# Graph attention on one core: order of the residual chain and of the finished rows in the last turns

## The reference

```python
x = _layernorm(x + L0(x))     # two GraphSAGE steps with mean over neighbours
# L1: attention over the edges, four heads of 128
alpha = einsum('ehd,ehd->eh', q[dst], k[src] + e) / sqrt(D)
attn = softmax of alpha over the edges of one destination
out = segment_sum((v[src] + e) * attn) + (x @ Wskip + bskip)
normed = (out - mu) * rsqrt(var + LN_EPS) * ln_g + ln_b
x = _layernorm(x + elu(normed @ Wlin + blin + x))
```

## Time and profile before

| what | value |
|---|---|
| median of 3 runs | 1611.04 us |
| lowest and highest run | 1610.73 and 1617.06 us |
| the profiled execution's own time | 1612.87 us |
| its span | 1610.7 us |
| mean granted clock of TensorE | 0.977 of full speed |

### The profile page before, as it was taken

One profiled execution on the slowest core, in us unless ns is written; L12 is line 12 of the kernel. 1 busy time (PEld: TensorE's weight loads), 2 busy tenths in 40 slices (PEclk: granted clock), 3 DMA queues, 4 the chain that ended last, 5 costly groups with the idle time before them and its releaser, 6 DMA issues. The chain is left out here.

```text
span 1610.7 us, 35668 instructions
## 1 busy us (share of the span) xinstructions
PE 1483.8 (92%) x8869; PEld 1135.5 (70%) x8869; DVE 1326.6 (82%) x6248; ACT 1169.2 (73%) x3273; POOL 1036.0 (64%) x1038
## 2 busy tenths in 40 slices
PE   4999999999999998999699977999999999999973
PEld 3777777777777776788566643777777777777763
DVE  5999999999999998566468865788888888888873
ACT  2999999999999998344257751677777777777763
POOL 3788888878888885677367727466566556655421
PEclk9999999999999999999989998999999999999997
DMA  2566666554444443233269963233333333333210
GB/s 80 147 161 159 159 162 162 155 159 150 150 150 150 152 150 119 73 92 92 58 197 288 291 214 97 81 91 91 90 89 87 88 91 90 90 90 88 67 41 6
DMA packets 148429, 199.22 MB, mean 124 GB/s; under 512 B 28399, under 2 KB 71582, under 8 KB 148310
## 3 DMA queue, kind: packets, MB, share of 16 engines
q1 hardware_dynamic: 119690, 160.01, 32.5%
q0 software_dynamic: 27200, 36.26, 10.0%
q10 hardware_dynamic: 1420, 1.60, 0.3%
HBM read 106.66 MB, written 100.07 MB: 128 GB/s over the span
## 5 line engine op out<-in xcount | busy, mean ns | idle before, releaser
L1371 POOL DMA_INDIRECT big<-x_tab,look x196 | 199.8, 1019 | 92.3 <-issue 58.6
L739 PEld LDWEIGHTS pb<-MG_s,big 128*128 128x128 f32 x832 | 149.5, 189 | 126.7 <-ACT big L772 110.5
L1388 POOL DMA_INDIRECT out_dram<-big,idx x98 | 100.5, 1026 | 210.6 <-PE pb L1466 73.4
L739 PE MATMUL pb<-MG_s,big 128*128 128x256 f32 x832 | 207.3, 392 | 24.7 <-ACT big L772 24.6
L748 ACT ACTIVATE big<-big 128x128 f32<-128x128 f32 x416 | 180.2, 482 | 0.0
L721 PE MATMUL pb<-C_s,big 128*128 128x128 f32 x832 | 161.8, 276 | 0.0
L722 PE MATMUL pb<-Ws1c_s,big 128*128 128x128 f32 x832 | 161.8, 276 | 0.0
L880 POOL TENSOR_TENSOR big<-big,cl 128x512 f32<-128x512 f32 x104 | 133.3, 1282 | 36.1 <-DVE big L844 34.0
L1689 DVE CUSTOM_DVE_ANT_0 big<-pb,big,zero 128x128 f32<-128x128 f32 x392 | 119.6, 345 | 38.7 <-PE pb L1511 38.3
L1442 PEld LDWEIGHTS pb<-big 128*128 128x128 f32 x792 | 103.9, 192 | 51.8 <-issue 37.7
L1121 POOL DMA_INDIRECT big<-h1e_tab,hidx x98 | 98.1, 1001 | 60.0 <-issue 35.5
(11 more groups left out here) (362 smaller groups left out, 4165.8 us busy)
## 6 DMA issues: line engine op xcount, KB each, us to landing
big<-in_x_dram SPq DMA_DIRECT2D x104, 256.0 KB
x_tab<-big SPq DMA_DIRECT2D x98, 256.0 KB
out_dram<-big SPq DMA_DIRECT2D x98, 256.0 KB, 2.1
c_ve<-ve_tab SPq DMA_DIRECT2D x98, 256.0 KB, 2.6
ve_tab<-c_ve SPq DMA_DIRECT2D x66, 256.0 KB, 3.6
h1e_tab<-a_rows SPq DMA_DIRECT2D x25, 256.0 KB, 2.6
x_tab<-a_rows SPq DMA_DIRECT2D x25, 256.0 KB
big<-in_edge_attr_dram SPq DMA_DIRECT2D x97, 64.0 KB, 1.8
```

The source lines that it names most:

```text
L739: t = pe.matmul(o, b_x1T[:, r * P:(r + 1) * P], MG_s[:], start=True, stop=True)
L1371: g.indirect_dma_start(out=o, out_offset=None, in_=x1_tab, in_offset=bass.IndirectOffsetOnAxis(ap=look[:, a, j:j + 1], axis=0), bounds_che ...
```

## The change

In turns that still have a new tile (`a < NT`) every engine's order stays as it was. In the turns without one (`a >= NT`) three things move:

- ScalarE does the exponential of tile d ahead of the squares of tile c, no longer behind them.
- VectorE does the residual chain of d (`final_sum`: L1813, L1817, L1819, L1821) directly behind the value sum and `d_z`, ahead of the compare of b and of the sum of squares of c. Before, it came behind both.
- ScalarE writes the finished rows of d last in its turn, behind the group's Exp (L1657) and the Ln and Exp of tile c (L1661, L1663). Before, they came ahead of these.

No instruction is added or taken away, and no wait has a new value.

```diff
# ScalarE
                 act.activation(d_ob[c % 2], OB[c % 2][:], ACT.Copy).then_inc(step("d_ob"), 1)
+
+            def squared(c):
+
                 after(act, "d_red", c - 1)
                 act.activation(d_sq, OB[c % 2][:], ACT.Square).then_inc(step("d_sq"), 1)
...
                 if live(c):
                     turned(c)
+                if live(c) and a < NT:
+                    squared(c)
                 if live(d):
                     exponential(d)
+                if live(c) and a >= NT:
+                    squared(c)
...
-                if live(d):
-                    after(act, "d_nm2", d)
-                    landed_before(act, dma_o[d % 4], d // 4)
-                    act.activation(d_out[d % 4], d_w[d % 2], ACT.Identity, scale=d_rs2,
-                                   bias=d_nm2[d % 2]).then_inc(step("d_o2"), 1)
+                if live(d) and a < NT:
+                    finished(d)
...
                     act.activation(d_rs[c % 2], d_lw, ACT.Exp, scale=-0.5).then_inc(step("d_rs"), 1)
+
+                if live(d) and a >= NT:
+                    finished(d)
# VectorE
                 if live(b) and a < NT:
                     value_sum(b)
+
+                if live(d) and a >= NT:
+                    final_sum(d)
 
                 if live(b):
                     v.tensor_scalar(d_same[b % 2], dst_row[:, b * P:(b + 1) * P], dst_f[:, b + 1:b + 2], None,
...
                 if live(c):
                     squares(c)
...
-                if live(d):
-                    after(v, "d_e", d)
-                    (the same four instructions)
+                if live(d) and a < NT:
+                    final_sum(d)
```

More of the change, by code:

```diff
@@ L1599, in exponential, with finished @@
                 act.activation(d_e, d_z[d % 2], ACT.Exp, bias=neg1[:, 0:1]).then_inc(step("d_e"), 1)
+            def finished(d):
+                after(act, "d_nm2", d)
+                landed_before(act, dma_o[d % 4], d // 4)
+                act.activation(d_out[d % 4], d_w[d % 2], ACT.Identity, scale=d_rs2,
+                               bias=d_nm2[d % 2]).then_inc(step("d_o2"), 1)
             for it in range(D_TURNS):
@@ L1780, in row_variance, with final_sum @@
                 v.tensor_scalar(d_var[c % 2], SB[:, 0:1], d_m2, 0.0, ALU.subtract, ALU.max).then_inc(step("d_var"), 1)
+            def final_sum(d):
+                after(v, "d_e", d)
+                v.scalar_tensor_tensor(out=d_t, in0=d_e, scalar=1.0, in1=d_z[d % 2], op0=ALU.min,
+                                       op1=ALU.max).then_inc(step("d_t"), 1)
+                after(v, "d_t", d)
+                after(v, "d_o2", d - 2)
+                v.tensor_tensor(d_w[d % 2], d_t, d_x1d[d % XD], ALU.add).then_inc(step("d_w"), 1)
+                after(v, "d_w", d)
+                v.bn_stats(d_st2, d_w[d % 2]).then_inc(step("d_s2"), 1)
+                after_apart(v, "d_s2", d)
+                v.bn_aggr(d_mv2[d % 2], d_st2).then_inc(step("d_bn2"), 1)
             for it in range(D_TURNS):
```

## The result

| | before | changed |
|---|---|---|
| median of 20 runs of each | 1611.63 us | 1618.64 us |
| lowest and highest run | 1609.72 and 1618.38 us | 1616.59 and 1621.72 us |
| profiled execution, span | 1610.7 us | 1615.9 us |
| from the copy of turn 98 to the end of the span | 89.0 us | 95.8 us |

The medians differ by 7.0 us. The ratio taken over all runs is 1.0037 (95% interval 1.0028 to 1.0046), by which the change costs 6.0 us (4.5 to 7.4). It is slower, by less than 0.5%. The forecast was +2.6 us, and 1618.64 us lies outside the stated range, which ended at 1617.4.

What follows compares the result with a forecast made beforehand. TensorE bounds the kernel before the drain, a circle of waits bounds the drain. 3.60 + 0.15 + 0.07 − 0.51 − 0.72 = +2.59 us on a median of 1611.04 gave 1613.6 us, range 1610.0 to 1617.4.

Steps and rivals of the forecast that it cites:

- circle: Drain turns: waits from ScalarE's copy through TensorE's sums, variance, Ln and Exp to the next copy, 5.44 us a turn.
- closing part: Behind turn 109: it hangs on the last finished rows and moves as a whole, with no change of length counted.
- Finished rows last: ScalarE, between Exp and next copy: 0.40 us newly paid in turns 98 to 104, 106 and 107, 3.60 us.
- an instruction put between them is paid in full: ScalarE: the next copy starts 0.11 us after the Exp with no other wait, so anything inserted delays it fully.
- Exponential ahead of the squares: ScalarE: squares now stand between exponential and Ln, 4.52 us in place of 4.37 in turn 98, +0.15 us.
- Turn 104's extra: VectorE's value sum stands behind three steps of the closing part in turn 104; estimated at +0.07 us.
- Where the residual chain was in the way: Turns 107 and 108: with the chain ahead on VectorE they gain 0.51 and 0.72 us.
- Residual chain ahead: VectorE: the compare behind the chain stays hidden under the weighting, so TensorE's sums are not late; 0, bound 3.1 us.
- my first rival: VectorE's compare waits for GpSimd's L1384, sums 0.18 us late in eight turns, 1.4 us more: 1615.0 us; chance 0.25.
- The clock: TensorE's clock falling in the drain: nothing in the sum; as a rival, slower by 14 us, 1628 us; chance 0.04.
- no new pause is as long as that of turn 105: Argument against a clock fall: turn 105's pause held TensorE over 2 us, and turn 103 kept full clock after 0.74.
- the rival: Every drain turn at TensorE's lower clock, 1.8 us in eight turns, 14 us; about three turns give 8.0; chance 0.04.

Runs made afterwards that it cites:

- changed_pool_late_pe_filled: Changed kernel with GpSimd's add held in the drain until VectorE's compare of the tile before, and TensorE's pauses filled with dummy transposes; timed 1.0010 (0.9988 to 1.0031).
- before_pe_filled: Kernel before with dummy transposes in TensorE's drain pauses (3 ahead of the products, 5 ahead of the sums, 14 in turn 106); timed 0.9997 (0.9977 to 1.0016).
- changed_sums_pause_filled: Changed kernel with 6 dummy transposes ahead of TensorE's sums from turn 99 on, none in turn 107 or ahead of the products; profiled once, not timed.
- changed_pe_filled: Changed kernel with 6 dummy transposes ahead of TensorE's products (14 in turn 106, 12 in 108) and 6 ahead of its sums, from turn 99; timed 1.0021.
- finished_last_pe_filled: Kernel before with only the finished rows moved last from turn 98 on, and TensorE's pauses filled with dummy transposes; timed 1.0003 (0.9979 to 1.0027).
- chain_first_pe_filled: Kernel before with only exponential and residual chain moved ahead from turn 98, TensorE's pauses filled, 36 dummy transposes ahead of the closing sums; timed 0.9992 (0.9969 to 1.0014).

## Why the prediction was wrong

Up to the Exp of turn 108, and then to the end, the two first profiles differ by:

| term | forecast | measured | from |
|---|---|---|---|
| circle without clock and without the slowed add | +2.59 | +2.55 | changed_pool_late_pe_filled less before_pe_filled |
| slowed add, sums late | 0 | +1.14 | changed_sums_pause_filled (61.45) less changed_pool_late_pe_filled (60.31) |
| turns at the lower clock, net | 0 | +4.27 | changed (66.40) less changed_sums_pause_filled, 4.95; less 0.68 in the kernel before |
| turn 108 at the lower clock | 0 | +0.23 | its Exp at T+4.44, not T+4.21 |
| closing part, nearly all its sums | 0 | −1.45 | −1.90 in the table's last column, less the −0.45 of turn 108's Exp |

The sum is +6.74 us, the profiles' difference from the copy of turn 98 on. In timed runs the loss was 6.0. The third term depends on the executions that are compared: the long turns cost 4.95 and 4.90 us in the two profiles of the changed kernel, and 0.68, 0.63 and 2.99 in the three with the order of before and no fills in the loop. For changed_pe_filled, whose closing part is as slow as before, the terms give 2.55 + 1.14 + 0.39 (its turn 107) − 0.68 = +3.4 us; timed were +3.4.

*Finished rows last.* Right in the steady turns, 0.38 against 0.40, with nothing in turn 105: the step "an instruction put between them is paid in full" held. Taken alone they cost less than the 3.60 of the sum, +2.64 (finished_last_pe_filled). In the turns 98 and 107 they add only 0.14 and 0.13, and turn 108 is 0.25 shorter, because in the old order they had held up the Ln there. The forecast had put that gain to the residual chain, which alone costs +0.66 (chain_first_pe_filled) where its terms come to −1.01. Only the sum of the two parts was forecast well, not what each is worth by itself.

*Exponential ahead of the squares.* Right in the new order. Turn 98 came to 6.95 in changed_pool_late_pe_filled; forecast were 6.39 + 0.40 + 0.15 = 6.94, and the way from the exponential to the Ln was 4.53, forecast 4.52. Turn 104's extra was 0.11, forecast 0.07.

*Where the residual chain was in the way.* Right: turn 107 from copy to copy 4.95 (forecast 4.98), turn 108 to the Exp 4.21 at full clock (forecast 4.17).

*Residual chain ahead.* Wrong in size. I asked what GpSimd would do to the compare only, and took 0. The compare kept its 0.26; it never met GpSimd's add, so whether it would have waited in full, as the Trainium skill (SBUF — State Buffer, section "Who interferes with whom") has it, was not seen. The victim was the add of the chain itself, ahead of it: an instruction with two inputs in SBUF that now stood where GpSimd's own add was queued. The sums came 0.19 later in the turns 102, 103, 105 and 106, with all else at full speed, and hardly later in the others: +1.14 us. That is near my first rival (0.18 a turn, 1.4 in all), by another instruction; its agreement in size is luck.

*The clock.* This is the step that failed most: the falls of TensorE's clock were put at nothing, and measured +4.27 us net. The forecast left them out of the sum, and as a rival they got 0.04, because "no new pause is as long as that of turn 105". The runs show that this was no test: the changed kernel lost the clock in turn 102 with no pause over 0.96 us in that turn and the one before, and with six transposes a turn it kept it through a pause of 2.19. Nor did it fall in every turn, as the rival had it, which made 14 us. In each of its two profiles three of the turns 98 to 107 are hit, for 1.4 to 1.9 us each, and which ones changes from one execution to the next. The kernel before pays in turn 106 too, and was seen to pay in turn 99. Three turns are what the rival called enough for 8 us; it came to less, because the kernel before pays as well and the closing part gave 1.45 us back.

*The closing part.* Wrong too: it did not "move as a whole" but got 1.45 us shorter, since its sums ran at the higher level. Two errors of the clock thus stand against each other, and without this one the miss would have been larger.

What stays open is what makes the clock fall in one turn and not in its like, and how often the kernel before loses the clock ahead of turn 106 over many executions: it did in one of three profiles that have its order and no fills in the loop. The changed kernel did in both of its profiles.

## What to carry to other kernels

An instruction moved to where its queue does not wait is paid in full, even if it was free where it stood: look for the engine's idle time ahead of the step that ends last, and leave the work there. When a chain is moved on VectorE, lay GpSimd's instructions over each of its members, not only over the last one. Where TensorE is bound by waits, a longer turn can be charged twice, as here, once by the wait and once by the clock. Filling pauses with dummy transposes separates the two in one run. Whether the fills are worth keeping was not shown by the timed runs here.

## What was not expected of the hardware

- TensorE's granted clock fell in turn 102 of the changed kernel, where no pause since the start of turn 101 was over 0.96 us, and did not fall behind a pause of 2.19 us when six transposes (0.82 us) had been put into each turn.
- A VectorE add of 128x128 with both inputs in SBUF took 0.43 to 0.59 us in place of 0.29 while GpSimd's add stood next in its queue, although in the turns 99 to 106 GpSimd's record begins only after it.
- Two profiles of the kernel before, from two rounds, have the same turns 99 to 105 to 0.01 us, while their spans are 1610.7 and 1656.6 us; that difference lies ahead of the drain.
